# A gated feed-forward kernel on one core: the last store of the output is halved by partitions and sent from two queues

## The chip, the core and the metric

The kernel runs on one core of one Trainium2 chip. The metric is the device time of one execution in microseconds (us); lower is better. The kernel before takes 80.19 us, the median of three runs (80.17 to 80.28).

## The reference

```python
def reference(x, itok, cond_weights, w_gate, w_up, w_down):
    # x [32, 32, 256], itok [32], cond_weights [200, 32, 32]
    y = jnp.einsum('bct,bcd->bdt', x, cond_weights[itok])     # mix by condition
    h = jax.nn.silu(y @ w_gate) * (y @ w_up)                  # 256 -> 1024
    h_sparse = keep_two_largest_of_every_four(h)              # by absolute value
    return x + h_sparse @ w_down                              # 1024 -> 256
```

All data are float32. The output has 32 x 32 tokens of 256 features, 1 MB.

## The kernel before

The 1024 tokens lie along the free axis, in two halves of 512 (`TH`). Features lie on the partitions: the 256 features are two groups `k` of 128 (`KT` = 2), and the 1024 inner features are two groups `q` of four `j` of 128. Each matrix product is done as three products of high and low parts, so that the sum keeps float32's precision. The work on TensorE runs from the mixing (L550, L564) over 16 pairs of gate and up products (L579) to the down products (L621). VectorE multiplies, compares and masks, ScalarE takes silu, absolute values and the high parts.

Every engine has its own program, and the order in it is written out by hand; engines wait for one another through semaphores. Nothing is reordered by a scheduler.

The end of the program is what the change touches. The output `out` has the shape [128 partitions, k, 1024 tokens]. The tile `xt_sb` holds x in that layout (it lies in the space of `gate_raw`, and the profile calls it so); `output(i)` on VectorE (L455) adds the result of the down products to a block of it in place, and a store then sends the block. The list `OUTPUTS` (L169) names six such blocks:

```python
OUTPUTS = [(0, 0, 0, TH, y_banks[:, 0]), (0, 1, 0, TH, y_banks[:, 1]),
           (1, 0, 0, TH, gate_bank(ACC_PAIR)), (1, 1, 0, TH, up_bank(ACC_PAIR)),
           (1, 1, 0, TH // 2, gate_bank(PAIRS - 1)), (1, 1, TH // 2, TH, up_bank(PAIRS - 1))]
UNFINISHED, LEFT = 3, 4
```

Blocks 0, 1 and 2 are 128 x 512 and are stored whole from SP's queue. Block 3 is only a partial sum and isn't stored. Blocks 4 and 5 are the left and the right half of the columns of the last 128 x 512; block 4 (`LEFT`) is stored from ScalarE's queue, block 5 from SP's. Each step of VectorE raises `out_done` by one, the queue that stores block i waits for `out_done` to reach i + 1, and each store raises `stored` by 16 when it has landed. SP's last instruction of the program waits for `stored` to reach 80, five stores; the block's common end at L48 follows.

Of the kernel before, what the change touches and what calls it, by code (L numbers as in the profile page):

```python
# [10 lines left out]
def adaln_ffn(nc: bass.Bass, x: bass.AP, x_t: bass.AP, cond: bass.AP, table: bass.AP,  # L11
# [11 lines left out]
    P = 128  # L23
    i32 = mybir.dt.int32
    _, _, GH, T = x.shape
# [7 lines left out]
    TH = B * D // NH  # L33
# [14 lines left out]
    with ctx:  # L48
# [3 lines left out]
        def sem(name):  # L52
            return ctx.enter_context(nc.semaphore(name))
# [19 lines left out]
        xt_sb = raw_w[0].rearrange("p q k n -> p (q k n)").rearrange("p (k t) -> p k t", k=KT)  # L73
# [24 lines left out]
        def source(i):  # L98

            q, w, k, _, j, _ = PIECES[i]  # L100
            if q == 1:
                return second_in[w], 32
            if j == 2:
                return rest_in[w], 16
            return (first_in[k], 16) if w == 0 else (up_in, 16)
# [26 lines left out]
        out_done = sem("out_done")  # L132
# [10 lines left out]
        stored = sem("stored")  # L143
# [3 lines left out]
        def gate_bank(n):  # L147
            return banks[:, GATE_BANKS[n % RING]]

        def up_bank(n):  # L150
            return banks[:, UP_BANKS[n % RING]]
# [6 lines left out]
        def split_y(part, half, k, end):  # L158
# [10 lines left out]
# [4 lines that stand above are left out]
# [7 lines left out]
        def raw_piece(i):  # L180
            q, w, k, end, j, j_end = PIECES[i]
            return raw_w[w][:, q, k:end].rearrange("p k (j g) -> p k j g", j=M)[:, :, j:j_end]

        def split_piece(i, part):
            q, w, k, end, j, j_end = PIECES[i]
            return w_hl[w][:, part, q, k:end, j:j_end]

        @block.sync
        def _(sp):
            sp.dma_start(cond_sb[:], cond).then_inc(cond_in, 16)  # L190

            sp.dma_start(x_sb[:, 0:GH, :], x[0]).then_inc(x_in[0], 16)
            sp.dma_start(raw_w[0][:, 0, 0, 0:2 * P], w_gate[0, 0, 0]).then_inc(first_in[0], 16)

            sp.wait_ge(mix_in[0], 16)
            for k in range(1, KT):
                sp.dma_start(raw_w[0][:, 0, k, 0:2 * P], w_gate[0, 0, k]).then_inc(first_in[k], 16)
            sp.dma_start(raw_w[1][:, 0, :, 0:2 * P], w_up[0, 0].rearrange("k p n -> p k n")).then_inc(up_in, 16)
            for w, weights in enumerate((w_gate, w_up)):
                sp.dma_start(raw_w[w][:, 0, :, 2 * P:4 * P],  # L200
                             weights[0, 1].rearrange("k p n -> p k n")).then_inc(rest_in[w], 16)
            sp.wait_ge(up_in, 16)
            sp.dma_start(x_sb[:, GH:NG, :], x[1]).then_inc(x_in[1], 16)
            for w, weights in enumerate((w_gate, w_up)):
                for i in range(2):
                    sp.dma_start(raw_w[w][:, 1, :, 2 * i * P:2 * (i + 1) * P],
                                 weights[1, i].rearrange("k p n -> p k n")).then_inc(second_in[w], 16)
            sp.dma_start(down_raw[:], w_down).then_inc(down_in, 16)
            sp.wait_ge(w_hi, GATE_PIECES_END)
            sp.wait_ge(w_lo, GATE_PIECES_END)  # L210
            sp.dma_start(xt_sb, x_t).then_inc(xt_in, 16)
            for i, (half, k, begin, end, _) in enumerate(OUTPUTS):
                if i not in (UNFINISHED, LEFT):
                    cols = slice(half * TH + begin, half * TH + end)
                    sp.wait_ge(out_done, i + 1)
                    sp.dma_start(out[:, k, cols], xt_sb[:, k, cols]).then_inc(stored, 16)
            sp.wait_ge(stored, 16 * (len(OUTPUTS) - 1))

        @block.gpsimd
        def _(pool):  # L220
# [28 lines left out]
        @block.scalar  # L249
        def _(act):  # L250

            def high_weights(i):
                act.wait_ge(*source(i))
                nc.scalar.activation(split_piece(i, HI), raw_piece(i), ACT.Copy).then_inc(w_hi, 1)  # L254

            def high_y(half, k, end):
                act.wait_ge(mixed, KT * half + end)
                nc.scalar.activation(split_y(HI, half, k, end), mixed_y(half, k, end), ACT.Copy).then_inc(y_hi, 1)  # L258

            def gate_silu(n):  # L260
                act.wait_ge(pair_done, n + 1)
                if n >= 3:
                    act.wait_ge(h_done, n - 2)
                nc.scalar.activation(silu[:, n % 3], gate_bank(n), ACT.Silu).then_inc(silu_done, 1)  # L264

            def absolute(n):
                u, j = divmod(n, M)
                act.wait_ge(h_done, n + 1)
                if j == 0 and u >= 2:
                    act.wait_ge(masked, M * (u - 2) + 1)  # L270
                nc.scalar.activation(a[u % 2][:, j], hs[u][:, j], ACT.Abs).then_inc(abs_done, 1)  # L271

            def high_down(q):
                act.wait_ge(down_in, 16)
                nc.scalar.activation(down_hl[:, HI, q].rearrange("p j t -> p (j t)"), down_raw[:, q],
                                     ACT.Copy).then_inc(down_hi, 1)

            def negative_down(q):
                act.wait_ge(down_in, 16)
                nc.scalar.activation(down_hl[:, LO, q].rearrange("p j t -> p (j t)"), down_raw[:, q],  # L280
                                     ACT.Copy, scale=-1.0).then_inc(down_neg, 1)

            def high_h(u, j, end):
                act.wait_ge(masked, M * u + end)
                nc.scalar.activation(h_hl[:, u, HI, j:end], hs[u][:, j:end], ACT.Copy).then_inc(h_hi, 1)  # L285

            def negative_h(u, j, end):
                act.wait_ge(masked, M * u + end)
                nc.scalar.activation(h_hl[:, u, LO, j:end], hs[u][:, j:end], ACT.Copy,  # L289
                                     scale=-1.0).then_inc(h_neg, 1)  # L290

            act.wait_ge(warm_zero, 1)
            nc.scalar.activation(silu[:, 0, 0:2], warm[:, 0:2], ACT.Silu).then_inc(table_loaded, 1)
            for k in range(KT):
                high_weights(k)
                high_y(*Y_PIECES[k])
            for i in range(KT, LATER):
                high_weights(i)
            act.wait_ge(table_loaded, 1)
            gate_silu(0)  # L300
            gate_silu(1)
            absolute(0)
            high_weights(LATER)
            gate_silu(2)
            absolute(1)
            high_weights(LATER + 1)
            high_y(*Y_PIECES[KT])
            absolute(2)
            gate_silu(3)
            absolute(3)  # L310
            gate_silu(4)
            gate_silu(5)
            absolute(4)
            negative_down(0)
            gate_silu(6)
            absolute(5)
            gate_silu(7)
            high_h(0, 0, 2)
            absolute(6)
            absolute(7)  # L320
            gate_silu(8)
            negative_h(0, 0, 2)
            negative_down(1)
            gate_silu(9)
            high_down(0)
            high_h(0, 2, 4)
            absolute(8)
            gate_silu(10)
            negative_h(0, 2, 4)
            absolute(9)  # L330
            gate_silu(11)
            high_down(1)
            gate_silu(12)
            absolute(10)
            absolute(11)
            high_h(1, 0, 2)
            gate_silu(13)
            absolute(12)
            high_h(1, 2, 4)
            gate_silu(14)  # L340
            negative_h(1, 0, 2)
            absolute(13)
            negative_h(1, 2, 4)
            gate_silu(15)
            absolute(14)
            absolute(15)
            high_h(2, 0, 2)
            high_h(2, 2, 4)
            high_h(3, 0, 1)
            high_h(3, 1, 2)  # L350
            high_h(3, 2, 3)
            high_h(3, 3, 4)
            half, k, begin, end, _ = OUTPUTS[LEFT]
            cols = slice(half * TH + begin, half * TH + end)
            act.wait_ge(out_done, LEFT + 1)
            act.dma_start(out[:, k, cols], xt_sb[:, k, cols]).then_inc(stored, 16)

        @block.vector
        def _(dve):
# [336 lines left out]
```

## Time and profile before

| | |
|---|---|
| median of three runs | 80.19 us (80.17 to 80.28) |
| profiled execution, its own time | 80.31 us |
| its span | 78.4 us, 1027 instructions |
| outside the span | 1.9 us |
| TensorE busy | 73.9 us (94%) |
| VectorE busy | 62.7 us (80%) |
| ScalarE busy | 42.1 us (54%) |
| GpSimd busy | 8.1 us (10%) |
| TensorE's granted clock | 1.0 throughout |
| HBM read, written | 5.38 MB, 1.05 MB |

The span runs from the first to the last instruction in the trace; the execution's own time is longer by what lies around it. Engine names in rows: PE is TensorE, DVE is VectorE, ACT is ScalarE, SP is the queue engine; a q behind a name (SPq, ACTq) marks instructions of its sequencer, such as the issue of a DMA. q1 is the DMA queue that SP feeds, q10 the one that ScalarE feeds.

### The profile page before, as it was taken

What the parts mean: (1) busy time and instruction counts of PE and PEld (TensorE: products, weight loads), DVE (VectorE), ACT (ScalarE), POOL (GpSimd) and SP (SyncE); (2) the same over time, 40 slices, a digit from 0 to 9 for tenths busy, and PEclk for the clock granted to TensorE, in tenths of its full rate; (3) what the DMA queues carried; (4) which work ended last, traced back from release to release, by engine and by line L of the source; (5) the groups of instructions that cost most, each with busy time, mean ns of one, the idle gap of its engine ahead of it and who ended that gap; (6) DMA issues with size and microseconds to landing.
All of it is one profiled execution on the core that took longest, in us unless ns stands there. A gap on an engine that the chain in (4) does not pass through costs nothing.

```text
span 78.4 us, 1027 instructions
## 1 busy us (share of the span) xinstructions
PE 73.9 (94%) x362; PEld 59.6 (76%) x362; DVE 62.7 (80%) x93; ACT 42.1 (54%) x62; POOL 8.1 (10%) x17
## 2 busy tenths in 40 slices
PE   3988999999999999999999999999999999999950
PEld 1328888888888888888888888888888888888840
DVE  1006884689889999599999979999999999994460
ACT  6122773799443465699897769798380402720000
POOL 3460000000000013000804000006200000000000
PEclk9999999999999999999999999999999999999999
DMA  0726979995910005900199990003994000003333
GB/s 1 273 95 168 286 234 318 302 418 180 410 67 0 0 0 98 169 0 0 36 196 199 184 192 8 4 0 67 201 180 88 0 0 0 8 0 140 135 134 126
DMA packets 4565, 9.64 MB, mean 123 GB/s; under 512 B 560, under 2 KB 2864, under 8 KB 4304
## 3 DMA queue, kind: packets, MB, share of 16 engines
q1 hardware_dynamic: 3488, 6.16, 23.0%
q0 software_dynamic: 928, 3.28, 21.9%
q10 hardware_dynamic: 144, 0.13, 0.5%
q8 instruction: 3, 0.05, 0.3%
q14 instruction: 2, 0.02, 0.1%
HBM read 5.38 MB, written 1.05 MB: 82 GB/s over the span
## 4 chain that ended last, share of the span: by engine, by line
PE 94%; issue 1%; DVE 1%
PE banks L579 52%; PE banks L621 28%; PE banks L541 6%; PE banks L564 4%; PE banks L591 3%; PE banks L550 1%; DVE gate_raw L455 1%; DVE warm L458 0%
## 5 line engine op out<-in xcount | busy, mean ns | idle before, releaser
L579 PE MATMUL banks<-y_hl,up_hl 128*128 128x512 f32 x96 | 24.2, 389 | 0.0
L621 PE MATMUL banks<-h_hl,down_hl 128*128 128x512 f32 (+1 forms) x102 | 22.0, 376 | 0.0
L579 PE MATMUL banks<-y_hl,gate_hl 128*128 128x512 f32 x84 | 21.4, 390 | 0.0
L621 PEld LDWEIGHTS banks<-h_hl,down_hl 128*128 128x128 f32 x102 | 18.5, 188 | 3.6
L579 PEld LDWEIGHTS banks<-y_hl,up_hl 128*128 128x128 f32 x96 | 18.0, 188 | 3.8
L579 PEld LDWEIGHTS banks<-y_hl,gate_hl 128*128 128x128 f32 x84 | 15.7, 188 | 3.2
L264 ACT ACTIVATE silu<-banks 128x512 f32<-128x512 f32 x16 | 9.6, 597 | 11.1 <-PE banks L579 10.8
L404 DVE TENSOR_TENSOR h<-banks,silu 128x512 f32<-128x512 f32 x12 | 8.2, 687 | 3.8 <-ACT silu L264 3.7
L285 ACT ACTIVATE h_hl<-h 128x1024 fp32r<-128x1024 f32 (+1 forms) x8 | 6.7, 842 | 3.9 <-DVE h L440 3.9
L440 DVE SCALAR_TENSOR_TENSOR h<-count,h 128x512 f32<-128x512 bf16 x12 | 7.9, 685 | 0.1
L271 ACT ACTIVATE x_sb<-h 128x512 f32<-128x512 f32 x8 | 4.9, 625 | 1.7 <-DVE h L404 1.7
L541 PE MATMUL banks<-warm 128*128 128x512 bf16 x12 | 4.5, 550 | 1.2 <-DVE warm L458 1.2
L455 DVE TENSOR_TENSOR gate_raw<-banks,gate_raw 128x512 f32<-128x512 f32 (+1 forms) x6 | 3.5, 598 | 2.4 <-PE banks L621 2.3
L240 POOL DMA_DIRECT2D h_hl<-h x4 | 3.7, 928 | 13.4 <-ACT h_hl L289 13.4
L235 POOL DMA_DIRECT2D down_hl<-down_raw x2 | 1.8, 919 | 31.2 <-ACT down_hl L280 31.2
L415 DVE TENSOR_TENSOR far<-x_sb 128x1024 bf16<-128x1024 f32 x4 | 4.9, 1220 | 0.2
L415 DVE TENSOR_TENSOR far<-a_even 128x1024 bf16<-128x1024 f32 x4 | 4.9, 1220 | 0.2
L541 PEld LDWEIGHTS banks<-warm 128*128 128x128 bf16 x12 | 1.5, 134 | 3.6 <-issue 2.2
L254 ACT ACTIVATE gate_hl<-gate_raw 128x256 fp32r<-128x256 f32 (+2 forms) x4 | 2.5, 632 | 3.2 <-DMA gate_raw<-in_w_gate 3.1
L289 ACT ACTIVATE h_hl<-h 128x1024 fp32r<-128x1024 f32 x4 | 4.2, 1056 | 0.0
L285 ACT ACTIVATE h_hl<-up_raw 128x1024 fp32r<-128x1024 f32 x2 | 2.1, 1054 | 3.2 <-DVE up_raw L440 3.2
L258 ACT ACTIVATE y_hl<-banks 128x512 fp32r<-128x512 f32 (+1 forms) x3 | 2.2, 737 | 2.1 <-PE banks L550 2.0
(39 smaller groups left out, 66.7 us busy)
## 6 DMA issues: line engine op xcount, KB each, us to landing
h_hl<-h POOLq DMA_DIRECT2D x4, 512.0 KB, 6.1
x_sb<-in_x SPq DMA_DIRECT2D x2, 512.0 KB, 3.7
up_raw<-in_w_up SPq DMA_DIRECT2D x4, 256.0 KB, 4.3
down_raw<-in_w_down SPq DMA_DIRECT2D x1, 1024.0 KB, 7.6
gate_raw<-in_x_t SPq DMA_DIRECT2D x1, 1024.0 KB, 5.9
down_hl<-down_raw POOLq DMA_DIRECT2D x2, 512.0 KB, 4.9
gate_raw<-in_w_gate SPq DMA_DIRECT2D x3, 256.0 KB, 4.1
out<-gate_raw SPq DMA_DIRECT2D x3, 256.0 KB, 2.3
```

Source lines behind the costliest of these rows:

```text
L240: pool.dma_start(h_hl[:, u, LO, j:end], hs[u][:, j:end], accum_op=ALU.add).then_inc(h_lo_sent[u][j // 2], 16)
L264: nc.scalar.activation(silu[:, n % 3], gate_bank(n), ACT.Silu).then_inc(silu_done, 1)
L271: nc.scalar.activation(a[u % 2][:, j], hs[u][:, j], ACT.Abs).then_inc(abs_done, 1)
L285: nc.scalar.activation(h_hl[:, u, HI, j:end], hs[u][:, j:end], ACT.Copy).then_inc(h_hi, 1)
L289: nc.scalar.activation(h_hl[:, u, LO, j:end], hs[u][:, j:end], ACT.Copy, scale=-1.0).then_inc(h_neg, 1)
L404: nc.vector.tensor_tensor(hs[u][:, j], up_bank(n), silu[:, n % 3], ALU.mult).then_inc(h_done, 1)
L415: step(nc.vector.tensor_tensor(far[:, j - 2::2], au[:, 0:2], au[:, j:j + 1].broadcast_to([P, 2, TH]), ALU.is_ge))
L440: nc.vector.scalar_tensor_tensor(hs[u][:, j], count[:, j], bound, hs[u][:, j], op, ALU.mult).then_inc(masked, 1)
L455: nc.vector.tensor_tensor(xt_sb[:, k, cols], bank[:, begin:end], xt_sb[:, k, cols], ALU.add).then_inc(out_done, 1)
L541: nc.tensor.matmul(gate_bank(0), warm[:, 0:P], warm[:], start=True, stop=True)
L579: last = nc.tensor.matmul(dst, w_hl[w][:, s, q, k, j], y_hl[:, m, half, k], start=i == 0, stop=i == len(terms) - 1)
L621: last = nc.tensor.matmul(bank[:, begin:end], down_hl[:, s, q, j, k * P:(k + 1) * P], h_hl[:, u, m, j, begin:end], start=(q, j, m, s) == f ...
```

## The change

Block 5, the last one stored, is sent in two DMAs instead of one. SP sends partitions 0 to 63 of it, and ScalarE, after its own store of block 4, waits for the same step of VectorE and sends partitions 64 to 127. The last wait of SP is for six stores in place of five. No computation is changed.

```diff
@@ SP's program
                 if i not in (UNFINISHED, LEFT):
                     cols = slice(half * TH + begin, half * TH + end)
+
+                    rows = slice(0, P // 2 if i == LEFT + 1 else P)
                     sp.wait_ge(out_done, i + 1)
-                    sp.dma_start(out[:, k, cols], xt_sb[:, k, cols]).then_inc(stored, 16)
-            sp.wait_ge(stored, 16 * (len(OUTPUTS) - 1))
+                    sp.dma_start(out[rows, k, cols], xt_sb[rows, k, cols]).then_inc(stored, 16)
+            sp.wait_ge(stored, 16 * len(OUTPUTS))
@@ ScalarE's program
             act.wait_ge(out_done, LEFT + 1)
             act.dma_start(out[:, k, cols], xt_sb[:, k, cols]).then_inc(stored, 16)
+            half, k, begin, end, _ = OUTPUTS[LEFT + 1]
+            cols = slice(half * TH + begin, half * TH + end)
+            act.wait_ge(out_done, LEFT + 2)
+            act.dma_start(out[P // 2:P, k, cols], xt_sb[P // 2:P, k, cols]).then_inc(stored, 16)
```

The end of ScalarE's program before: the last activations, the store of block 4, and the branch to the common end.

```order
52 L285 ACTIVATE h_hl<-up_raw 128x1024 x2
53 L285 ACTIVATE h_hl<-h 128x512 x4
54 L356 DMA out<-gate_raw 128x256
55 L48 UNCONDITIONAL_BRANCH
```

The same place in the changed kernel, whose line numbers are larger by 2:

```order
52 L287 ACTIVATE h_hl<-up_raw 128x1024 x2
53 L287 ACTIVATE h_hl<-h 128x512 x4
54 L358 DMA out<-gate_raw 128x256
55 L362 DMA out<-gate_raw 64x256
56 L48 UNCONDITIONAL_BRANCH
```

One DMA of 64 partitions has come behind the store of block 4; nothing ahead of it moved.

The end of SP's program before:

```order
12 L211 DMA gate_raw<-in_x_t 128x2048
13 L216 DMA out<-gate_raw 128x512 x3
14 L216 DMA out<-gate_raw 128x256
15 L48 UNCONDITIONAL_BRANCH
```

And in the changed kernel:

```order
12 L211 DMA gate_raw<-in_x_t 128x2048
13 L218 DMA out<-gate_raw 128x512 x3
14 L218 DMA out<-gate_raw 64x256
15 L48 UNCONDITIONAL_BRANCH
```

The last store keeps its place and has half the partitions. No instruction of TensorE, VectorE or GpSimd changes.

## Rows read from the trace of the kernel before

**Rows 1.** The chain that ended last, in order of time: start us, us, what.

```profile
core 0 of [0], span 78.4 us
...
53.83 21.84 PE banks L621 x102
...
75.69 0.42 DVE gate_raw L455
```

**Rows 2.** Timeline of 75.6 to 78.4 us: start us, us, engine, instruction.

```profile
75.52 0.37 ACTq L356 DMA_DIRECT2D out<-gate_raw  x1
75.69 0.42 DVE L455 TENSOR_TENSOR gate_raw<-banks,gate_raw 128x256 f32<-128x256 f32 x1 [0.21 <-PE banks L621]
76.14 0.33 SPq L216 DMA_DIRECT2D out<-gate_raw  x1
```

**Rows 3.** Page, DMA issues: KB each, median us from issue to landing.

```profile
out<-gate_raw SPq DMA_DIRECT2D x3, 256.0 KB, 2.3
...
out<-gate_raw ACTq DMA_DIRECT2D x1, 128.0 KB, 1.9
out<-gate_raw SPq DMA_DIRECT2D x1, 128.0 KB, 1.9
...
cond_sb<-in_cond SPq DMA_DIRECT2D x1, 2.0 KB, 1.8
```

**Rows 4.** Instructions of line 48, the common end: durations in ns, then starts.

```profile
L48 ACTq DRAIN  x1: 153/153/153, 75.9 to 75.9; - x1
L48 SPq COMPARE_BRANCH  x1: 33/33/33, 78.0 to 78.0; - x1
...
L48 SPq EVENT_SEMAPHORE  x1: 17/17/17, 78.4 to 78.4; - x1
```

**Rows 5.** What SP waited for, 75.9 to 78.4 us: total, times, longest.

```profile
SPq L48 <- DMA out<-gate_raw: 1.6, 1, 1.6
```

**Rows 6.** Stretches: busy us of each engine, clock, DMA share of 16 engines, GB/s.

```profile
76.35:76.40 0.05, 0.00 (x0) 0.00 (x0) 0.00 (x0) 0.00 (x0) 0.00 (x0) 1.00 0.24 82
...
76.85:76.90 0.05, 0.00 (x0) 0.00 (x0) 0.00 (x0) 0.00 (x0) 0.00 (x0) 1.00 0.10 21
76.90:76.95 0.05, 0.00 (x0) 0.00 (x0) 0.00 (x0) 0.00 (x0) 0.00 (x0) 1.00 0.00 0
76.95:77.00 0.05, 0.00 (x0) 0.00 (x0) 0.00 (x0) 0.00 (x0) 0.00 (x0) 1.00 0.24 82
...
77.20:77.30 0.10, 0.00 (x0) 0.00 (x0) 0.00 (x0) 0.00 (x0) 0.00 (x0) 1.00 1.04 358
...
77.45:77.50 0.05, 0.00 (x0) 0.00 (x0) 0.00 (x0) 0.00 (x0) 0.00 (x0) 1.00 0.02 0
77.50:77.55 0.05, 0.00 (x0) 0.00 (x0) 0.00 (x0) 0.00 (x0) 0.00 (x0) 1.00 0.00 0
```

**Rows 7.** DMA view, 76 to 78.4 us: packets, MB, share of 16 engines.

```profile
DMA packets 288, 0.26 MB, mean 109 GB/s; under 512 B 32, under 2 KB 288, under 8 KB 288
...
q10 hardware_dynamic: 144, 0.13, 16.3%
q1 hardware_dynamic: 144, 0.13, 16.2%
```

**Rows 8.** Timeline of SP, 0 to 24 us: how its DMA issues follow each other.

```profile
0.75 0.38 SPq L190 DMA_DIRECT2D cond_sb<-in_cond  x1
1.19 0.42 SPq L192 DMA_DIRECT2D x_sb<-in_x  x1
1.66 0.42 SPq L193 DMA_DIRECT2D gate_raw<-in_w_gate  x1
5.72 0.33 SPq L197 DMA_DIRECT2D gate_raw<-in_w_gate  x1
6.09 0.44 SPq L198 DMA_DIRECT2D up_raw<-in_w_up  x1
6.57 0.47 SPq L200 DMA_DIRECT2D gate_raw<-in_w_gate  x1
```

## The prediction

> **What bounds the kernel now.** I read the chain that ended last first. Over the whole span it is TensorE's, and it leaves TensorE only at the end, for the last addition on VectorE, 0.42 us from 75.69 to 76.11 [rows 1]. The change adds and removes nothing ahead of that point: all that runs on TensorE, VectorE and GpSimd, and everything on SP and ScalarE up to their last instruction, stays as it is. So only the tail counts, from 76.11 to the span's end at 78.4, some 2.3 us.
>
> The tail is read from four views. The timeline shows the order of issue: ScalarE starts its store of block 4 at 75.52 and is through at 75.89, before VectorE has ended block 5; SP starts the store of block 5 at 76.14, 0.03 after VectorE's end, and is through 0.33 later [rows 2]. The narrow stretches show when data moved. The 1 KB rows of block 4 run from within 76.35-76.40 to within 76.85-76.90, the engines are idle to 76.95, and then come those of block 5, to shortly after 77.45 [rows 6]. The issues' landing times say that both stores of 128 KB are counted as landed 1.9 us after their issue began, SP's at 78.04 [rows 3], and the branch behind SP's last wait is at 78.0, the last semaphore instruction at 78.4 [rows 4]. The waits confirm that SP waits 1.6 us for this DMA and for nothing else [rows 5].
>
> So the tail is a sum of five: 0.03 to wake SP, 0.33 of issue, some 0.5 from the end of the issue to the first packet (76.47 to about 76.96), some 0.5 of moving data (to about 77.46), some 0.55 from the last packet to the landing, and then 0.4 of the common end. The reader is to see that the moving of data is only a fifth of it, and that the rest doesn't depend on bytes in an evident way: a transfer of 2 KB lands after 1.8 us, one of 128 KB after 1.9, one of 256 KB after 2.3 [rows 3].
>
> **The change part by part.** The sum is made against the profiled execution, 80.31 us (78.4 of span and 1.9 around it). It is 0.12 above the median of the runs, 80.19, so I work out a difference and add it to 80.19.
>
> *SP's issue.* It covers 64 partitions in place of 128. No row has an issue of 64, so I bound it. Below: the issue costs by the row of data, and halves, -0.17. Above: it has a fixed cost, 0. The rows say which is nearer. A first issue after a pause takes 0.33 for 128 rows of 1 KB; an issue right behind another takes 0.42 with 128 rows (both issues at 1.19 and 1.66) and 0.44 to 0.47 with 256 pieces [rows 8] (the loads at 6.09 and 6.57 take two pieces of 1 KB for each partition). So 128 pieces more cost 0.02 to 0.05, and 64 fewer save 0.01 to 0.03. I take -0.02.
>
> *ScalarE's issue.* It is new, and it is on the path, as SP now waits for both halves. ScalarE is free: its store of block 4 is issued by 75.89, and VectorE ends at 76.11 [rows 2], so the wait that is added has nothing queued behind it but the common end. That end's drain on ScalarE moves from 75.9 [rows 4] to about 76.5, and is hidden by the 1.5 us to 78.0; with no such cover it would cost its 0.15. ScalarE's issue took 0.37 against SP's 0.33 [rows 2], so its half reaches the DMA engines 0.04 later, or 0.14 later if an issue so soon behind another costs the 0.10 more that SP's do [rows 8]. What a late second half costs follows from the next term.
>
> *Moving the data.* 128 rows over 16 engines are 8 for each. q1 had 16.2% of 16 engines over 2.4 us, which is 0.39 us for each engine, for 8 rows and a small packet at the end, 9 packets in all [rows 7]; all 16 are busy, as the share of 1.04 shows [rows 6]. In halves, if each is spread over all 16 engines, an engine has 4 rows from SP's queue and 4 from ScalarE's: the same 8. The first four keep it busy for about 0.19. If the second half comes a time D after the first, the end moves by D - 0.19 when D is over 0.19, and not at all below. D of 0.04 or 0.14 costs nothing.
>
> *A second completion.* One small packet more for each engine (32 of the 288 packets are of this kind, 16 for each store). Bounds: 0, and the mean of all packets, 0.39/9 = 0.04. They carry nearly nothing, so I take +0.01.
>
> *The staggered start.* Data move for about 0.5 us (76.95-77.00 to 77.45-77.50, 0.45 to 0.55) though an engine is busy for 0.39, so the last engine starts 0.06 to 0.16 behind the first. With half the rows in each queue this may halve: between -0.08 and 0. The small ramp, 0.24 of 16 engines in the first 0.05 us, stands in both stores [rows 6]. I take 0, since the engines also share what is being started.
>
> *Landing and end.* The last packet still needs its 0.55 to be counted, and the 0.4 behind it stays: 0.
>
> Sum: -0.02 + 0 + 0 + 0.01 + 0 = -0.01, which is nothing. Predicted 80.19 - 0.01, rounded up a little for what a second queue may cost: 80.20 us.
>
> **The rivals.** *Slower: the two halves are started one after the other.* If what turns an issue into packets is shared, ScalarE's half comes behind SP's by the spacing of two issues in one queue: 0.37 (5.72 to 6.09) to 0.48 (6.09 to 6.57) [rows 8]. Then D - 0.19 is +0.18 to +0.29, and the time 80.37 to 80.48. It is decided at D = 0.19 + 0.16 = 0.35; below that it would not be told from no change. For it: SP's issues right behind each other do take 0.1 longer, as if something ahead of them were still busy. Against it: that spacing holds the sequencer's own 0.33 to 0.47 of work, which two sequencers do side by side. The trace has no two issues of SP and ScalarE at one time: 75.52 and 76.14 are 0.6 apart. Chance 0.15.
>
> The Trainium skill, DMA: Bandwidth & Descriptors, "Rules for kernel authors", speaks against this very change: two transfers to disjoint partition halves "serialize", both being spread over the same 16 engines. Read as sharing of engines this is the sum above, -0.01; read as one after the other it is this rival, 80.37 to 80.48. Its section "Queues, rings and completion order" says that SP and ScalarE have no descriptor generator of their own, which is the mechanism of this rival; no row of this trace shows it.
>
> *Slower: a transfer of 64 partitions uses fewer engines.* If both halves ran on the same 8 engines, each would have 16 rows, 0.78 in place of 0.39: +0.39, 80.58. If on 8 different ones each, 8 rows again, and only ScalarE's 0.04 is seen: 80.23, no change. No row has 64 partitions; all with 128 spread over 16 engines. Chance 0.04 for the first.
>
> *Faster: a start that goes by rows.* If issue and stagger both go by the number of rows, ScalarE's issue takes 0.185 in place of SP's 0.33 (-0.15) and the stagger gives up to 0.08: -0.23, 79.96. With one of them alone, 80.04 to 80.11, of which only the first reaches -0.15, about the bound. For it: 1 KB rows are many small pieces. Against it: the issue hardly changes from 128 to 256 pieces [rows 8]. Nor can the bytes help: a step of 128 KB is worth 0.4 between 128 and 256 KB [rows 3], but an engine's share of bytes isn't less than before. Chance 0.10.
>
> **How the numbers follow.** A change below 0.2%, 0.16 us, can't be told from none. The likeliest case has 0.70, with its own range 80.10 to 80.30 (the stagger's -0.08 below, a D up to 0.3 above). Faster has 0.10, the shared start 0.15, fewer engines 0.04, and 0.01 is left to anything else that slows. So faster by over 0.2% has 0.10; slower by over 0.2% has 0.15 + 0.04 = 0.19, the other 0.01 being as likely to end within it; and within 0.2% there is 0.71. The range of 80.04 to 80.42 takes in the likeliest case, half of the shared start and a part of the faster one, and leaves some 0.17 outside.
>
> **What would show it.** In the changed kernel's profile: ScalarE's second issue starts within 0.05 of SP's at 76.14 (right), or later (the step on ScalarE's being free is wrong). Both halves have 80 packets, 64 rows and 16 completions, and take together 0.39 to 0.41 of each engine; if the data end by 77.5, as before, the sum holds. Data of ScalarE's queue that start 0.35 or more behind SP's show the shared start. A share near 0.5 of 16 engines shows fewer engines. An SP issue of 0.2 shows the faster rival. The prediction is wrong above all if the time from the end of the issue to the first packet, or from the last packet to the landing, 1.05 us together, changes when two queues work at once, since no row here shows it.

## The result and the profile after

The changed kernel is slower: 80.90 us, the median of 12 runs (80.69 to 81.34), against 80.27 of 12 runs of the kernel before (80.11 to 80.84) beside them. The ratio is 1.0072 with a 95% interval of 1.0048 to 1.0095, so the change costs 0.58 us (0.39 to 0.76). The forecast was no change.

The profiled execution took 81.24 us with a span of 79.4, which is 0.34 above its kernel's median. A part of its distance to the execution before has nothing to do with the change, and has to be set aside first. The chain that ended last, in order of time, has at its start and end:

```profile
1.20 5.30 PE banks L547 x12
...
54.25 21.84 PE banks L627 x102
76.09 0.02 issue
76.11 0.42 DVE gate_raw L461
```

The down products take the same 21.84 us, but begin at 54.25 instead of 53.83, and the last addition ends at 76.53 instead of 76.11 [rows 1]. Nearly all of the 0.42 arise at the program's start, which the change doesn't touch: the first 12 warm-up products take 5.30 us here and 4.46 before, where 0.57 of idle time followed them, so the mixing begins 0.28 later (6.51 against 6.23), and it takes 1.21 instead of 1.09. Executions of one kernel differ there: among the kernels below, which all have this start, the last addition begins between 75.58 and 76.27 where TensorE's work is the same. So I compare tails: from the end of the last addition to the end of the span, 78.4 - 76.11 = 2.3 us before, and 79.4 - 76.53 = 2.9 here. The 0.6 of difference is the 0.58 of the runs.

The timeline of the changed kernel's tail (start us, us, engine, instruction):

```profile
76.11 0.42 DVE L461 TENSOR_TENSOR gate_raw<-banks,gate_raw 128x256 f32<-128x256 f32 x1 [0.21 <-PE banks L627]
76.57 0.53 SPq L218 DMA_DIRECT2D out<-gate_raw  x1
76.57 0.56 ACTq L362 DMA_DIRECT2D out<-gate_raw  x1
```

ScalarE is free in time, and both issues start 0.04 after the addition. But each takes about 0.2 longer than an issue before, 0.53 against 0.33 on SP and 0.56 against 0.37 on ScalarE [rows 2]. The DMA view lists the landing times of the two halves:

```profile
out<-gate_raw SPq DMA_DIRECT2D x1, 64.0 KB, 2.1
out<-gate_raw ACTq DMA_DIRECT2D x1, 64.0 KB, 2.5
```

Each carries 64 KB and lands later than the 128 KB did, after 2.1 and 2.5 us against 1.9 [rows 3]. When the data moved is seen in stretches of 0.05 us (before the last two columns, DMA share of 16 engines and GB/s, stands the granted clock):

```profile
77.65:77.70 0.05, 0.00 (x0) 0.00 (x0) 0.00 (x0) 0.00 (x0) 0.00 (x0) 1.00 0.00 0
77.70:77.75 0.05, 0.00 (x0) 0.00 (x0) 0.00 (x0) 0.00 (x0) 0.00 (x0) 1.00 0.06 20
...
78.40:78.45 0.05, 0.00 (x0) 0.00 (x0) 0.00 (x0) 0.00 (x0) 0.00 (x0) 1.00 0.16 41
78.45:78.50 0.05, 0.00 (x0) 0.00 (x0) 0.00 (x0) 0.00 (x0) 0.00 (x0) 1.00 0.01 0
```

The first data move 1.13 to 1.18 us after the issue began, where before it was 0.81 to 0.86 [rows 2, 6], and the movement lasts some 0.73 us instead of 0.5. The DMA view of the first 0.3 us of it shows one queue only:

```profile
DMA packets 47, 0.05 MB, mean 160 GB/s; under 512 B 0, under 2 KB 47, under 8 KB 47
...
q1 hardware_dynamic: 47, 0.05, 72.1%
```

From 77.70 to 78.00 nothing of q10 moves, while SP's half has 47 of its 80 packets done. ScalarE's half starts its data about 0.3 later than SP's though issued at the same moment, and so sets the end. The DMA view of 77.5 to 79.4 us has both halves whole:

```profile
q1 hardware_dynamic: 80, 0.07, 15.7%
q10 hardware_dynamic: 80, 0.07, 14.0%
```

Over these 1.9 us each of the 16 engines is busy for 0.30 us with SP's half and for 0.27 with ScalarE's, 0.56 together, where it was 0.39 for the same 128 rows in one store [rows 7]. The rows themselves have become slower. The instructions of the common end complete the picture:

```profile
L48 ACTq DRAIN  x1: 622/622/622, 77.2 to 77.2; - x1
L48 SPq COMPARE_BRANCH  x1: 33/33/33, 79.1 to 79.1; - x1
...
L48 SPq EVENT_SEMAPHORE  x1: 17/17/17, 79.4 to 79.4; - x1
```

ScalarE's drain has moved from 75.9 to 77.2 and takes 0.62 instead of 0.15, but it ends at 77.8 and is still hidden; from SP's branch to the end it is 0.3 to 0.4 as before [rows 4].

So the 0.6 are made of three observed parts: a start 0.32 later, a further 0.3 until ScalarE's half starts, and almost nothing back for its having half the rows: its data still move for 0.45 us, where the whole block took 0.5. The experiments ask what each belongs to.

### The profile page after: what moved, and what is told of

Its sections match the earlier page's. It is cut to its first block, busy times and chain, and to the rows that moved or that the text cites. A ratio compares the mean times of both kernels' runs of the same rounds, so it can differ in the third digit from the quotient of the medians.

```text
span 79.4 us, 1028 instructions
## 1 busy us (share of the span) xinstructions
PE 74.9 (94%) x362; PEld 59.8 (75%) x362; DVE 62.5 (79%) x93; ACT 41.7 (53%) x62; POOL 8.1 (10%) x17
## 4 chain that ended last, share of the span: by engine, by line
PE 94%; DVE 1%; issue 0%
PE banks L585 51%; PE banks L627 27%; PE banks L547 7%; PE banks L570 4%; PE banks L597 3%; PE banks L556 2%; DVE gate_raw L461 1%; DVE warm L464 0%
## 5 line engine op out<-in xcount | busy, mean ns | idle before, releaser
L266 ACT ACTIVATE silu<-banks 128x512 f32<-128x512 f32 x16 | 9.6, 597 | 11.8 <-PE banks L585 11.6
L547 PE MATMUL banks<-warm 128*128 128x512 bf16 x12 | 5.3, 632 | 1.2 <-DVE warm L464 1.2
L399 DVE TENSOR_TENSOR y_hl<-banks,y_hl 128x512 fp32r<-128x512 f32 (+1 forms) x3 | 2.6, 867 | 1.2 <-ACT y_hl L260 1.2
```

Of the source, the lines that this page charges most:

```text
L547: nc.tensor.matmul(gate_bank(0), warm[:, 0:P], warm[:], start=True, stop=True)
```

## The experiments

All tails are the span less the end of the last addition on VectorE, in us, each from the one profiled execution of its kernel. A tail leaves out the scatter of the program's start, which the times carry; the times rest on many runs; both are given. Differences in us are the ratio less one, times 80.3. Four theories were set against each other. A: two issues at one moment hinder each other. B: a second store so soon on ScalarE's queue is slow. C: a transfer of 64 partitions is slow by itself, in its start and in its rows; C1 lays the slow rows to which partitions they are, C2 to there being 64. D, later, asks which counts have the slow start: D1 64 alone, D2 all between 32 and 128.

| run | last block is sent as | ratio (95%) | tail |
|---|---|---|---|
| before | 128 partitions, SP | 1 | 2.3 |
| changed | 64 SP + 64 ScalarE | 1.0072 (1.0048 to 1.0095) | 2.9 |
| e1 | 128, ScalarE | 0.9991 (0.9972 to 1.0010) | 2.4 |
| e2 | 64 + 64, both SP | 1.0090 (1.0062 to 1.0117) | 3.2 |
| e3 | lower 64 only | 1.0017 (0.9995 to 1.0038) | 2.5 |
| e4 | 64 SP, 64 ScalarE 0.45 later | 1.0089 (1.0061 to 1.0116) | 2.9 to 3.0 |
| e5 | column halves, SP + ScalarE | 1.0020 (0.9998 to 1.0042) | 2.4 |
| e6 | left columns only | 0.9983 (0.9963 to 1.0004) | 2.1 |
| e7 | even 64 only | 1.0006 (0.9987 to 1.0026) | 2.4 |
| e8 | 128 SP, block 4 at the same moment | 1.0063 (1.0035 to 1.0091) | 2.8 |
| e9 | even SP + odd ScalarE | 1.0066 (1.0041 to 1.0092) | 2.7 |
| e10 | lower 32 only | 0.9969 (0.9951 to 0.9987) | 2.0 |
| e11 | last block of 128 columns | 1.0037 (1.0022 to 1.0053) | 2.5 |
| e12 | last block of 192 columns | 1.0019 (0.9997 to 1.0040) | 2.3 |
| e13 | lower 96 only | 1.0008 (0.9980 to 1.0036) | 2.3 |
| e14 | partitions 32 to 95 only | 1.0028 (1.0005 to 1.0052) | 2.6 |
| e15 | lower 64, left columns only | 0.9998 (0.9970 to 1.0026) | 2.4 |
| e16 | 96 SP + 32 ScalarE | 1.0028 (1.0001 to 1.0055) | 2.6 |

### e1: the whole block from ScalarE

```diff
-                if i not in (UNFINISHED, LEFT):
+                if i < UNFINISHED:
...
+            act.wait_ge(out_done, LEFT + 2)
+            act.dma_start(out[:, k, cols], xt_sb[:, k, cols]).then_inc(stored, 16)
```

> The last block goes whole, 128 partitions, from ScalarE's queue behind its store of block 4; SP stores blocks 0 to 2 only. Theory A (two issues at one moment hinder each other): there is one issue alone again, so ScalarE's second issue takes about 0.37 us as its first did, not 0.56, and the tail from VectorE's end to the span's end is 2.3 to 2.4 us, the time within 0.1 us of the kernel before. Theory B (a second store on ScalarE's queue 0.6 us behind its first is what costs): the issue takes 0.5 or more and the time stays near the changed kernel's, 0.4 to 0.6 us above the kernel before.

The timeline of the second issue, and the landing of both:

```profile
76.18 0.34 ACTq L360 DMA_DIRECT2D out<-gate_raw  x1
```

```profile
out<-gate_raw ACTq DMA_DIRECT2D x2, 128.0 KB, 1.9
```

The issue took 0.34, the time didn't move. Neither ScalarE's queue nor a second store on it so soon is what costs; theory B falls.

### e2: both halves from SP

```diff
-                    sp.dma_start(out[:, k, cols], xt_sb[:, k, cols]).then_inc(stored, 16)
+                    for rows in ([slice(0, P // 2), slice(P // 2, P)] if i == LEFT + 1 else [slice(0, P)]):
+                        sp.dma_start(out[rows, k, cols], xt_sb[rows, k, cols]).then_inc(stored, 16)
```

> Both halves by partitions are sent by SP, one behind the other. Theory A: no two issues at one moment; the second half's issue begins 0.37 to 0.48 us behind the first's and it moves 4 rows for each engine instead of 8, so the time is 0.2 to 0.35 us above the kernel before, less than the changed kernel's 0.6. Theory C (a store of 64 partitions is itself slow): the first half's landing already takes 2.1 us or more after its issue, and the time is 0.6 us or more above the kernel before.

The timeline shows SP's two issues as one row:

```profile
76.26 1.16 SPq L217 DMA_DIRECT2D out<-gate_raw  x2
```

SP waits for six stores here, as in the changed kernel. Two issues, one after the other, take 1.16 us with no second engine at work. This costs 0.72 us (0.50 to 0.94), no less than the changed kernel. Theory A alone can't give that, theory C can.

### e3: the lower 64 partitions alone

```diff
-                    sp.dma_start(out[:, k, cols], xt_sb[:, k, cols]).then_inc(stored, 16)
+                    rows = slice(0, P // 2 if i == LEFT + 1 else P)
+                    sp.dma_start(out[rows, k, cols], xt_sb[rows, k, cols]).then_inc(stored, 16)
```

> SP sends only the lower 64 partitions of the last block; the upper 64 of it are not stored at all, so this leaves out 64 KB of the output. It prices a store of 64 partitions alone. Theory A: the issue takes 0.31 to 0.33 us, data move for about 0.3 us instead of 0.5, the store lands 1.65 to 1.75 us after its issue and the time is 0.1 to 0.25 us below the kernel before. Theory C: landing takes 2.0 us or more and the time is at or above the kernel before's.

The timeline, the stretches in which the data start, and the DMA view of 77.20 to 77.75:

```profile
76.10 0.53 SPq L217 DMA_DIRECT2D out<-gate_raw  x1
```

```profile
77.20:77.25 0.05, 0.00 (x0) 0.00 (x0) 0.00 (x0) 0.00 (x0) 0.00 (x0) 1.00 0.00 0
77.25:77.30 0.05, 0.00 (x0) 0.00 (x0) 0.00 (x0) 0.00 (x0) 0.00 (x0) 1.00 0.36 82
```

```profile
q1 hardware_dynamic: 80, 0.07, 53.3%
```

With half the block left out and nothing else at work, the store is no faster than the whole (0.14 us slower, -0.04 to 0.31): issue 0.53, first data 1.15 to 1.20 after it, landing after 2.1. Each engine is busy for 0.533 x 0.55 = 0.29 us for 4 rows of data and the small packet at the end, where 8 rows took 0.39 [rows 7]. So 64 partitions are slow by themselves, in the start and in the rows. This is theory C, and the main finding.

### e4: ScalarE's half later

```diff
+        delayed = sem("delayed")
...
             act.wait_ge(out_done, LEFT + 2)
+            nc.scalar.activation(silu[:, 1, 0:TH // 2], warm[:, 0:TH // 2], ACT.Copy).then_inc(delayed, 1)
+            act.wait_ge(delayed, 1)
```

> The changed kernel, but ScalarE does an activation of 256 columns on a scratch tile, whose result nobody reads, and waits for it, between its wait for the last block and the issue of its half, so that its issue starts about 0.45 us later than SP's, when SP's is through. Theory A: both issues go back to 0.33 and 0.37 us, SP's half lands after about 1.7 us, ScalarE's about 1.7 to 1.8 us after its own, later, start, and the time is 0.2 to 0.35 us above the kernel before, so below the changed kernel although it starts its last store later. Theories B and C: the delay adds to what is there, 0.8 us or more above the kernel before.

```profile
76.54 0.54 ACTq L365 DMA_DIRECT2D out<-gate_raw  x1
```

```profile
out<-gate_raw SPq DMA_DIRECT2D x1, 64.0 KB, 2.1
out<-gate_raw ACTq DMA_DIRECT2D x1, 64.0 KB, 2.1
```

SP's issue runs from 76.09 to 76.62, so the two overlap for only 0.08, and ScalarE's still takes 0.54: theory A's account of the issue falls, as it did with e3, where there is one issue only. But ScalarE's half now lands 2.1 us after its issue instead of 2.5. The time is 0.71 us above the kernel before, a little under the 0.8 of theories B and C and far above theory A's 0.35: the delay of 0.45 costs only some 0.1 more than none (0.71 against 0.58, with intervals that overlap), as most of it was waited for anyway. So a second store at the same moment does lose 0.3 to 0.4, not in the issue, but behind it.

### e5 and e8: two stores of 128 partitions at one moment

e5 halves the block by columns. Its edit is shown against the changed kernel; both stores name all partitions again:

```diff
-                    rows = slice(0, P // 2 if i == LEFT + 1 else P)
+                    if i == LEFT + 1:
+                        cols = slice(half * TH + begin, half * TH + end - P)
...
-            cols = slice(half * TH + begin, half * TH + end)
+            cols = slice(half * TH + end - P, half * TH + end)
```

> The last block is halved by columns instead: SP sends its left 128 columns, ScalarE its right 128, both of all 128 partitions with rows of 512 B, issued at one moment. Theory C (64 partitions are what is slow, in the issue, in the start and in the rows): both issues take 0.33 to 0.38 us, the first data come about 0.83 us after the issue, and the time is within 0.15 us of the kernel before. Theory A (two issues at one moment hinder each other): issues of 0.5 us or more and the time 0.4 us or more above the kernel before.

e8 is the kernel before with block 4's store held back:

```diff
-            act.wait_ge(out_done, LEFT + 1)
+            act.wait_ge(out_done, LEFT + 2)
```

> The kernel before, but ScalarE's store of block 4 waits for block 5 too, so that it is issued at the same moment as SP's store of block 5; both have all 128 partitions. The last data then are 256 KB instead of 128. Theory C: issues of 0.33 and 0.37 us and a start after 0.83 us as before, only 16 rows for each engine instead of 8: 0.3 to 0.4 us above the kernel before, as a store of 256 KB stands to one of 128. Theory A: issues of 0.5 us or more, and 0.7 us or more above.

The timeline and the landings of e5:

```profile
76.72 0.33 SPq L219 DMA_DIRECT2D out<-gate_raw  x1
76.72 0.37 ACTq L363 DMA_DIRECT2D out<-gate_raw  x1
```

```profile
out<-gate_raw SPq DMA_DIRECT2D x1, 64.0 KB, 1.8
out<-gate_raw ACTq DMA_DIRECT2D x1, 64.0 KB, 2.0
```

and the landings of e8:

```profile
out<-gate_raw SPq DMA_DIRECT2D x1, 128.0 KB, 2.1
out<-gate_raw ACTq DMA_DIRECT2D x1, 128.0 KB, 2.4
```

Both issues are short again, 0.33 and 0.37. e5's half-size stores at one moment take a ratio of 1.0020, which can't be told from no change; this is what the prediction had expected of the change itself. e8 costs 0.51 us, 0.1 to 0.2 more than theory C's 0.3 to 0.4 for 256 KB in one transfer, and less than theory A's 0.7; its interval, 0.28 to 0.73, takes in both, and it is the short issues that speak against A. In these pairs ScalarE's store lands 0.2 to 0.4 behind SP's: 0.2 in e5, 0.3 in e8, 0.4 in the changed kernel. In the stretches of 0.05 us its data start 0.15 behind SP's in e5, 0.25 in e8 and 0.3 in the changed kernel. In none of the runs was ScalarE's the store that came first.

### e6: 64 KB from 128 partitions

```diff
+                    if i == LEFT + 1:
+                        cols = slice(half * TH + begin, half * TH + end - P)
                     sp.dma_start(out[:, k, cols], xt_sb[:, k, cols]).then_inc(stored, 16)
```

> SP sends only the left 128 of the 256 columns of the last block, from all 128 partitions: 64 KB as with the lower 64 partitions alone; the right 128 columns of it are not stored, so this leaves out 64 KB of the output. Theory C: issue 0.33 us, data move for 0.25 to 0.35 us, and the time is 0.1 to 0.25 us below the kernel before. If a store of 64 KB is slow by its size and not by its partitions, it behaves as the lower 64 partitions alone did: issue 0.53 us, time within 0.1 us of the kernel before.

```profile
out<-gate_raw SPq DMA_DIRECT2D x1, 64.0 KB, 1.7
```

The same 64 KB as e3, but landed after 1.7 instead of 2.1 us; the tail is 2.1 against 2.5. It is the shape that costs, not the size. The gain in time, 0.14, is within its interval of nothing.

### e7 and e14: which 64 partitions

```diff
-                    sp.dma_start(out[:, k, cols], xt_sb[:, k, cols]).then_inc(stored, 16)
+                    rows = slice(0, P, 2 if i == LEFT + 1 else 1)
+                    sp.dma_start(out[rows, k, cols], xt_sb[rows, k, cols]).then_inc(stored, 16)
```

> SP sends only the 64 even partitions of the last block (0, 2, 4 and so on); the odd ones are not stored, so this leaves out 64 KB of the output. Theory C1 (64 adjacent partitions are read through half of the paths that all 128 have, so that rows of 1 KB take 76 ns instead of 47): even partitions lie over all of them, rows take 47 to 60 ns on average and data move for 0.3 to 0.4 us. Theory C2 (any transfer of 64 rows has slow rows): 76 ns again, about 0.44 us. Under both the issue, if its 0.53 us comes from the count of partitions, stays at 0.53, and the time lies 0.05 to 0.1 us under the lower 64 alone under C1, and the same under C2.

e14 has `rows = slice(P // 4, 3 * P // 4)` in this place.

> SP sends only the partitions 32 to 95 of the last block; the others are not stored, so this leaves out 64 KB of the output. The range is 64 adjacent partitions like the lower half, but half of it lies below 64 and half above. Theory C1 in its narrow form (the partitions 0 to 63, 32 apart in pairs, are read over shared paths, and the two halves of 128 have paths of their own): rows go back to 47 ns as with the even partitions, data move for 0.33 us. If any 64 adjacent partitions are slow: 76 ns. The issue stays at 0.53 either way, and the time is within 0.15 us of the kernel before.

The DMA view of e7's last data, 77.50 to 77.95, then of e14's, 77.20 to 77.75:

```profile
q1 hardware_dynamic: 80, 0.07, 43.9%
```

```profile
q1 hardware_dynamic: 80, 0.07, 36.0%
```

An engine is busy for 0.439 x 0.45 = 0.20 us with the even partitions and for 0.360 x 0.55 = 0.20 with 32 to 95, against 0.29 with 0 to 63. The rows themselves, in the trace's records of single packets, have a median of 46 ns in both and of 76 in e3. So the slow rows belong to the position of the partitions and not to there being 64, which the narrow form of C1 fits. Its pairing 32 apart is not tested by itself: the lower 32 alone (e10) have no such pairs, and their rows have a median of 56. The issues stay long, 0.54 and 0.59. The times don't follow the rows: e14 is 0.22 us above the kernel before (0.04 to 0.42), outside the 0.15 expected, and e7 0.05 (-0.10 to 0.21). The slow start, which all three share, outweighs what the faster rows give back.

The Trainium skill, SBUF — State Buffer, "Door 1: The DMA port swizzle", says that the partitions from 0 to 63 reach only 8 of the 16 ports that DMA reads through. By its table both 32 to 95 and the even ones reach all 16; the busy times above agree with it.

### e9: even and odd halves

```diff
-                    rows = slice(0, P // 2 if i == LEFT + 1 else P)
+                    rows = slice(0, P, 2 if i == LEFT + 1 else 1)
...
-            act.dma_start(out[P // 2:P, k, cols], xt_sb[P // 2:P, k, cols]).then_inc(stored, 16)
+            act.dma_start(out[1:P:2, k, cols], xt_sb[1:P:2, k, cols]).then_inc(stored, 16)
```

> The changed kernel, but the last block is halved into even partitions (SP) and odd partitions (ScalarE) instead of lower and upper; both issued at one moment. Both halves have 64 partitions, so the issue of 0.53 us and the start 0.3 us later stay; ScalarE's data start 0.3 us behind SP's as in the changed kernel. Only the rows should go back from 76 ns to 47 (theory C1). Sum from the runs: 0.32 for the start, 0.30 for ScalarE's half, 0.33 of its data against 0.53 before: 0.42 us above the kernel before, 0.1 to 0.2 us below the changed kernel. If the position of the partitions doesn't matter when two queues work, the time equals the changed kernel's, 0.6 above.

```profile
out<-gate_raw SPq DMA_DIRECT2D x1, 64.0 KB, 2.0
out<-gate_raw ACTq DMA_DIRECT2D x1, 64.0 KB, 2.3
```

Both landings are 0.1 to 0.2 shorter than in the changed kernel, and the tail is 2.7 against 2.9, as the theory of rows has it. In the DMA view of 77.5 to 79.2 us the queues have 12.0% and 11.6%, so an engine is busy for 0.40 us with both halves instead of 0.56, and the data move from 77.75 to about 78.35, for 0.6 instead of 0.73, though ScalarE's still start 0.25 behind SP's. The runs don't confirm it: 0.53 above the kernel before against 0.58, with intervals that overlap almost wholly. The size of this part in the time stays open, between 0 and 0.2.

### e10, e13 and e15: which counts have the long start

The three send `slice(0, P // 4)`, `slice(0, 3 * P // 4)`, and the lower 64 with the left 128 columns only.

> SP sends only the lower 32 partitions of the last block; the other 96 are not stored, so this leaves out 96 KB of the output. It asks whether the long issue belongs to 64 partitions or to any count below 128, and whether it grows or shrinks with the count. If it is the price of leaving the full 128, the issue is again about 0.53 us and the data start 1.15 us after it; rows stay slow, 76 ns, with 2 for each engine, so the store lands about 1.95 us after its issue and the time is that of the kernel before, within 0.1 us. If the issue goes by rows, 0.3 us or less.

> SP sends only partitions 0 to 95 of the last block; the upper 32 are not stored, so this leaves out 32 KB of the output. Stores of 128 and of 32 partitions issued in 0.33 us and started their data after 0.82, stores of 64 needed 0.53 and 1.15. Theory D1 (64 adjacent or spaced partitions are a case of their own): 96 issues in 0.33 us and the time is within 0.15 us of the kernel before. Theory D2 (every count between 32 and 128 is slow): 0.5 us or more, start after 1.1, and 0.1 to 0.4 us above the kernel before.

> SP sends the lower 64 partitions and only the left 128 of the 256 columns of the last block, 32 KB in rows of 512 B; the rest of the block is not stored, so this leaves out 96 KB of the output. The bytes are those of the lower 32 partitions with full rows, which issued in 0.34 us and came 0.26 us below the kernel before. If the long issue goes with the count of 64, it is again 0.53 us with a start after 1.15, and the time is within 0.1 us of the kernel before; if it goes with the bytes, 0.34 and 0.2 us or more below.

The timelines of e10, e13 and e15, in this order:

```profile
76.13 0.34 SPq L217 DMA_DIRECT2D out<-gate_raw  x1
```

```profile
76.03 0.35 SPq L217 DMA_DIRECT2D out<-gate_raw  x1
```

```profile
76.64 0.53 SPq L219 DMA_DIRECT2D out<-gate_raw  x1
```

And the stretches in which the data of e10 and of e13 start:

```profile
76.90:76.95 0.05, 0.00 (x0) 0.00 (x0) 0.00 (x0) 0.00 (x0) 0.00 (x0) 1.00 0.00 0
76.95:77.00 0.05, 0.00 (x0) 0.00 (x0) 0.00 (x0) 0.00 (x0) 0.00 (x0) 1.00 0.49 123
```

```profile
76.80:76.85 0.05, 0.00 (x0) 0.00 (x0) 0.00 (x0) 0.00 (x0) 0.00 (x0) 1.00 0.00 0
76.85:76.90 0.05, 0.00 (x0) 0.00 (x0) 0.00 (x0) 0.00 (x0) 0.00 (x0) 1.00 0.27 82
```

32 and 96 partitions issue in 0.34 and 0.35 us and start their data after 0.82 to 0.87, as 128 do. 64 partitions issue in 0.53 with rows half as long too. So it is neither the bytes nor being below 128: of the counts tried, 32, 64, 96 and 128, the count 64 alone is slow, in every one of the eight kernels that had it. For e10 I had named two cases, as slow as 64 or an issue of 0.3 us or less, and neither came: it issues in 0.34 and is 0.25 us faster than the kernel before (0.10 to 0.39). Counts other than these four weren't tried, and why 64 is slow no run tells.

### e16: the change, cut at 96

```diff
-                    rows = slice(0, P // 2 if i == LEFT + 1 else P)
+                    rows = slice(0, 3 * P // 4 if i == LEFT + 1 else P)
...
-            act.dma_start(out[P // 2:P, k, cols], xt_sb[P // 2:P, k, cols]).then_inc(stored, 16)
+            act.dma_start(out[3 * P // 4:P, k, cols], xt_sb[3 * P // 4:P, k, cols]).then_inc(stored, 16)
```

> The changed kernel with the last block cut at partition 96 instead of 64: SP sends 96 partitions, ScalarE 32, both issued at one moment; no transfer has 64 partitions. Theory D1: both issues in 0.33 to 0.37 us, the start after 0.82 and for ScalarE up to 0.13 later, so that the time is 0 to 0.2 us above the kernel before and 0.3 us or more below the changed kernel. Theory D2: 0.4 us or more above the kernel before.

```profile
76.08 0.35 SPq L218 DMA_DIRECT2D out<-gate_raw  x1
76.08 0.38 ACTq L362 DMA_DIRECT2D out<-gate_raw  x1
```

```profile
out<-gate_raw SPq DMA_DIRECT2D x1, 96.0 KB, 1.9
out<-gate_raw ACTq DMA_DIRECT2D x1, 32.0 KB, 2.1
```

With no transfer of 64 partitions the issues are short, and the cost is 0.22 us (0.01 to 0.44) instead of 0.58; the tail is 2.6 against 2.9. What is left is in the moving of data: it starts at 76.90 to 76.95, 0.82 to 0.87 after the issue, as before, but lasts 0.7 us instead of 0.5. Two things go together there that this run doesn't part: ScalarE's data start 0.25 behind SP's, and an engine is busy for 0.49 us instead of 0.39 (22.0% and 5.8% of 1.75 us in the DMA view).

### e11 and e12: another cut, in search of a faster tail

```diff
-                   (1, 1, 0, TH // 2, gate_bank(PAIRS - 1)), (1, 1, TH // 2, TH, up_bank(PAIRS - 1))]
+                   (1, 1, 0, TH - P, gate_bank(PAIRS - 1)), (1, 1, TH - P, TH, up_bank(PAIRS - 1))]
```

P is 128; e12 has 192 in its place.

> The kernel before with another cut of the last 512 columns: block 4 has 384 and block 5 has 128 in place of 256 each, both of all 128 partitions, block 4 from ScalarE's queue, block 5 from SP's. VectorE's last addition should take 0.25 to 0.3 us instead of 0.42, and the last store lands 1.7 us after its issue instead of 1.9. If nothing else becomes late, 0.15 to 0.35 us below the kernel before. Against it: block 4's 192 KB start later and both stores' data now meet; if these set the end, no change.

> As the run before, but block 4 has 320 columns and block 5 has 192. VectorE's last addition 0.33 to 0.36 us; 0.05 to 0.2 us below the kernel before, between it and the cut at 128 if block 5's chain sets the end, and the better of the two if block 4's data do.

The chain of e11 ends with:

```profile
54.25 22.09 PE banks L621 x102
76.35 0.02 issue
76.37 0.29 DVE gate_raw L455
```

The last addition is shorter, 0.29 against 0.42, but the down products take 22.09 instead of 21.84, and the last store lands 2.1 us after its issue, and not the 1.7 of e6's equal store: its first data come 1.01 to 1.06 us after the issue, while block 4's 192 KB are still moving. Both outweigh the gain: e11 is 0.30 us slower (0.18 to 0.43), e12 not to be told from the kernel before; a gain was expected of both. No version tried that stores the whole output beats the kernel before.

## Why the prediction was wrong

The prediction was 80.20 us with a range of 80.04 to 80.42 and a chance of 0.71 for no change; measured were 80.90, 0.58 us (0.39 to 0.76) above the kernel before.

*What bounds the kernel* was right: only the tail changed, and its terms are the ones to compare (it calls them five; they are six, and add up to the 2.3 us).

*SP's issue* is the step that failed. It said -0.02 with "Above: it has a fixed cost, 0". It measured +0.20, and behind it another +0.12 until the first data, a stretch for which the sum had no term at all: +0.32. The bounds were drawn from issues of 128 partitions only, and I took the cost to be monotonic in the count, between that of 128 and half of it. It isn't: 32, 96 and 128 cost 0.33 to 0.35, and 64 costs 0.53. The prediction named this gap at its end, "changes when two queues work at once", but put it down to two queues; e3 shows it with one.

*ScalarE's issue*: ScalarE was free and started with SP, as said. That its half comes 0.04 to 0.14 later was too small: it was 0.3, and the landing was 0.2 to 0.4 behind SP's in all five pairs (e5, e8, e9, e16 and the changed kernel). The rival "started one after the other" was in part right: D was 0.3, below its 0.37 to 0.48 and the 0.35 named as its sign. Without a transfer of 64 partitions two stores at one moment cost 0.22 in e16 and 0.16, unclear, in e5; the late half is only a part of these too, as an engine is busy there for 0.49 and 0.47 us in place of 0.39. No run shows the mechanism of this delay. That the two queues have no descriptor generator of their own, as the Trainium skill says in DMA: Bandwidth & Descriptors, "Queues, rings and completion order", would fit it.

*Moving the data*: 8 rows an engine in two halves was right, but not that they take the same 0.39 us. 4 rows took 0.29 in e3, and the two halves of the changed kernel 0.56, not the 0.39 to 0.41 that the prediction named as its sign. This is a mis-sized term: the data move for 0.73 us instead of 0.5. e9 has the same late start of ScalarE's data, but its rows are fast (0.40 for both halves, as predicted), and its data move for 0.6. So of the 0.23 some 0.1 goes with the late half, near the D - 0.19 of the prediction, and some 0.13 with the slow rows of adjacent partitions. That is read from one profiled execution of each; the times of the two kernels don't tell them apart.

*The second completion* and *landing and end* hold to within 0.1: from the last data to the branch it is 0.6 us, 78.5 to 79.1, against 0.5 before, 77.5 to 78.0.

*Fewer engines* and *faster by rows* didn't happen; 16 completions and 64 rows came from each half as said.

The sum made anew for the changed kernel: +0.32 for the start, +0.3 until the second half starts, -0.05 for its 0.45 of data in place of 0.5, which is 0.57, against 0.58 measured. That the two agree so closely is in part luck, as each term is read to 0.05 and the interval of the 0.58 is 0.39 to 0.76.

The Trainium skill's advice against halves of partitions (DMA: Bandwidth & Descriptors, "Rules for kernel authors") was the better forecast, but its reason, that the halves serialize, is only a part of what the runs show: the halves of the changed kernel overlap from 78.00 to 78.20, those of e5 and e16 for longer, and the long start of 64 partitions, 0.32 us, comes without any second half.

## What to carry to other kernels

Most of the time of a small last store doesn't go with its bytes: half of them took 0.2 us off the tail with all 128 partitions kept (e6; in the runs 0.14, not clear of nothing), and nothing with 64 partitions (e3, e7, e14). Sending one small store as two from two queues gained nothing in any form tried. By columns it cost least (0.16, not clear of nothing), with 64 partitions in each part most. Holding the second store back didn't help either (e4), nor did holding back an earlier store until the last one is issued (e8, 0.51 slower). An operation's cost at half size must be read from a row of that size: where there is none, the cost at full size is no upper bound.

## What was unexpected of the hardware

- A store of 64 partitions issues in 0.53 to 0.59 us, on SP and on ScalarE, and from SP its first data move 1.13 to 1.25 us after the issue begins; stores of 32, 96 and 128 partitions issue in 0.33 to 0.38, and with no other store's data moving their first data come after 0.80 to 0.87.
- Rows of 1 KB took 76 ns in the median from partitions 0 to 63, and 46 from 32 to 95 or from the even ones.
- Of two stores issued at one moment, ScalarE's lands 0.2 to 0.4 us behind SP's, in all five pairs.
- With six products of 128 columns and six of 384 in place of twelve of 256, the 102 down products took 22.09 us instead of 21.84 (e11).
